# A feed-forward stream started one unit later beside the attention, with new shares of work and the other engines' part of each slice one piece later

## The chip, the cores and the metric

The kernel runs as one program on one core of a Trainium2 chip. The metric is the device time of one execution, in microseconds; the time before is the median of three runs. The engines are TensorE (PE in the profile; its weight loads are PEld), VectorE (DVE), ScalarE (ACT), GpSimd (POOL) and SyncE (SP, which only issues DMAs here). Each engine works through its own instructions in order; between engines there are semaphores, set and waited for by hand.

## The reference

The input is 8 batch entries (b = 0 to 7) of 512 tokens of width 256, fp32. Per entry four residual blocks follow each other, each on the layer norm of its input:

```
x = x + attn_a(layernorm(x))    # state-space scan: 8 heads, state 64 x 64, rotation by dt, gate, rms norm
x = x + ffn(layernorm(x))       # silu(x w1) * (x w2) -> gelu(. h1) -> gelu(. h2) -> . w3, hidden width 1024
x = x + attn_b(layernorm(x))    # delta rule: 8 heads of 32, then layer norm of its output
x = x + ffn(layernorm(x))       # the same weights again
```

The entries don't depend on each other.

## The kernel before

**Attention.** Both attention blocks work on tiles of 128 tokens, four per entry. The state-space block ("SSM stage") has 8 steps per tile, 32 in all. In a tile: transposes of the normed tile (step 0), projections (1), decay sums, angles and exponentials (2), transposes of the rotated rows (3), scores (4), products with the values and the state (5), transposes (6), output projection and residual (7). The delta block ("delta stage") has 89 steps: D1, four tiles of 5 steps (projections and Gram matrices); the inversion, 31 steps, each a product and a subtraction on VectorE alone (lines 1079 and 1081); two steps ("gap") in which the inverse goes out to DRAM and comes back as `tbd`; D2, four tiles of 9 steps, a chain of small matmuls on TensorE and small operations on VectorE. SyncE moves the Gram matrices through DRAM (`a_scr`, then `au`) ahead of the inversion, and `ti` through `t_scr` into `tbd` behind it.

**Feed-forward.** A pass `p` over one entry is two units of 256 tokens, a unit 18 slices, numbered on through the pass. In a unit: slices 0 to 7 are the first layer (w1 and w2, 8 matmuls of 256 columns each), 8 to 11 the layer h1 and 12 to 15 the layer h2 (32 matmuls each), 16 the transposes of the next unit's input (`xt`, 4), 17 the product with w3 (32). Values are split in a high and a low part, hence twice the matmuls. A slice of TensorE's work ends in one of four PSUM banks `F`. The other engines' part of it follows. For the first layer: ACT silu to `gate`, DVE product to `hid` and cast to the high part (lines 899, 903), POOL the low part `hA_lo` (line 580). For the hidden layers: ACT two gelus and the cast (702, 703, 706), POOL the low part. For slice 16: ACT and DVE make `xf_hi` and `xf_lo`. For slice 17: DVE scales and adds to x and takes its statistics (922, 925, 851). The first matmuls of a layer wait for the low parts of the layer before, its last two blocks of 128 as late as possible (line 1218 waits on `f_lo`).

**The order.** `window` weaves a stage with a stream of slices by a plan: for each step of the attention a number of slices. All engines run the same plan, so each has a fixed order. In the code the attention's operations of a step come first, then slices up to the running sum `done`. TensorE's slice s begins at position s and has its second half at s + 0.5; the other engines' part stands at s + 0.5 and is emitted as soon as `done` exceeds that:

```
def window(attention, ffn, plan):
    att, mlp, done = Steps(attention), Steps(ffn), 0
    for step, slices in enumerate(plan):
        att.before(step + 1)
        done += slices
        mlp.before(done)
```

`spread` makes a plan from shares. By it the delta plan has 15 slices in D1 (8, 2.5, 2, 2.5 by tile), 10 in the inversion, 1.5 in the gap, 9.5 in D2; the SSM plan has 36 (11.5, 6.5, 11.5, 6.5 by tile). These counts are worked out from the code.

**The loop.** SSM stage of entry 0 alone; SSM stage of entry 1 with pass 0; then for b = 1 to 6 one iteration: delta stage of entry b - 1 with pass 2b - 1 (entry b after its SSM stage), then SSM stage of entry b + 1 with pass 2b (entry b - 1 after its delta stage); then delta stages 6 and 7 with a pass each, and a last pass alone. Each window holds whole passes, so a unit's input is the result of the stage just before. SyncE issues, per iteration: load of entry b + 1 (after the store of entry b - 2 has landed), the DMAs of the delta stage, store of entry b - 1.

## Time and profile before

| | |
|---|---|
| runs | 3176.04, 3181.72, 3186.53 us; median 3181.72 |
| profiled execution, own time | 3179.42 us |
| its span, first to last instruction | 3177.4 us |
| mean granted TensorE clock | 0.891 of full speed |
| busy: PE, DVE, ACT, POOL | 78%, 47%, 36%, 29% |
| one pass of the loop (mean of 6) | 385.2 us |

The span is what the engines' records cover; the own time has some 2 us around it. A line of a window has: stretch, its length, busy us and number of instructions of PE, PEld, DVE, ACT and POOL, granted TensorE clock as a share of full speed, DMA share, GB/s. A busy share is a mean over stages with different limits, so it is read stage by stage: a window of the trace gives the busy time of each engine, the number of its instructions and the granted clock in that stretch. A wait belongs to the engine in front of it; the releaser named is the one that ended it.

### The profile page before, as it was taken

How to read it: one execution, taken by the hardware profiler on the slowest of the kernel's cores; microseconds unless marked ns; L12 is line 12 of the kernel's file. 1: busy time of each engine (PE TensorE's matmuls, PEld its weight loads, DVE VectorE, ACT ScalarE, POOL GpSimd, SP SyncE). 2: the span in 40 equal slices, each digit the busy share in tenths (PEclk: the TensorE clock that was granted, in tenths of full speed). 3: DMA queues.
4: the chain of work that ended last, by engine and by line, in shares of the span. 5: the costliest groups of instructions: out<-in, count | busy, mean ns of one | idle time of the engine just before them, and what ended most of it. 6: DMA issues, size and time to landing. Idle time of an engine off the chain costs nothing.

```text
span 3177.4 us, 54420 instructions
## 1 busy us (share of the span) xinstructions
PE 2491.4 (78%) x20928; PEld 2195.7 (69%) x20928; DVE 1483.2 (47%) x3604; ACT 1157.8 (36%) x2426; POOL 926.0 (29%) x1216
## 2 busy tenths in 40 slices
PE   4678868888688886888868888678877888777688
PEld 3567757777577775787657776568766777666578
DVE  3434553445534445444454444545444444544541
ACT  2235432445225442245412544134432354323223
POOL 2123323233223232233323223232322233233233
PEclk7679988999799997999979998789987999898799
DMA  6000000000000000000000000000000000000000
GB/s 202 1 1 1 3 12 15 1 1 18 19 7 1 1 18 21 4 1 1 20 21 3 1 8 21 14 1 1 15 14 14 1 1 10 12 15 6 21 10 7
DMA packets 86976, 43.33 MB, mean 14 GB/s; under 512 B 71472, under 2 KB 81584, under 8 KB 86704
## 3 DMA queue, kind: packets, MB, share of 16 engines
q1 hardware_dynamic: 83040, 28.12, 3.5%
q0 software_dynamic: 3664, 11.53, 1.1%
q8 instruction: 177, 2.90, 0.4%
q14 instruction: 95, 0.78, 0.1%
HBM read 27.05 MB, written 12.58 MB: 12 GB/s over the span
## 4 chain that ended last, share of the span: by engine, by line
PE 46%; DVE 25%; ACT 10%; issue 10%; POOL 5%; DMA 3%; SPq 1%; DVEq 0%; POOLq 0%; ACTq 0%
PE F L1218 21%; DVE prod L1079 4%; DVE ti L1081 3%; PE Q L1261 3%; PE F L1240 2%; PE Q L1329 2%; PE Q L1346 2%; PE Q L1308 2%; POOL hA_lo L580 2%; DVE hid L899 2%; PE Q L1444 2%; PE Q L1414 1%; PE Q L1381 1%; PE Q L1300 1%; PE Q L1312 1%
## 5 line engine op out<-in xcount | busy, mean ns | idle before, releaser
L1218 PE MATMUL F<-hA_hi,h_sb 128*128 128x256 f32 x2048 | 568.1, 311 | 107.8 <-POOL hA_lo L580 107.4
L580 POOL TENSOR_TENSOR hA_lo<-hid,hA_hi 128x256 fp32r<-128x256 f32 (+1 forms) x384 | 353.0, 920 | 879.2 <-ACT hA_hi L706 494.0
L1218 PE MATMUL F<-hA_lo,h_sb 128*128 128x256 f32 x2048 | 542.9, 299 | 0.0
L1218 PE MATMUL F<-hB_hi,h_sb 128*128 128x256 f32 x2048 | 526.1, 295 | 0.3
L1218 PEld LDWEIGHTS F<-hA_hi,h_sb 128*128 128x128 f32 x2048 | 426.6, 208 | 127.9 <-POOL hA_lo L580 115.4
L1218 PE MATMUL F<-hB_lo,h_sb 128*128 128x256 f32 x2048 | 508.8, 287 | 0.0
L1198 PE MATMUL F<-xf_hi,w_sb 128*128 128x256 f32 x1024 | 319.0, 338 | 162.6 <-DVEq L902 69.2
L1218 PEld LDWEIGHTS F<-hA_lo,h_sb 128*128 128x128 f32 x2048 | 428.3, 209 | 0.5
L1218 PEld LDWEIGHTS F<-hB_hi,h_sb 128*128 128x128 f32 x2048 | 400.8, 196 | 19.0 <-issue 15.3
L1218 PEld LDWEIGHTS F<-hB_lo,h_sb 128*128 128x128 f32 x2048 | 401.7, 196 | 0.3
L1198 PEld LDWEIGHTS F<-xf_hi,w_sb 128*128 128x128 f32 x1024 | 234.9, 229 | 183.8 <-DVEq L902 82.9
L702 ACT ACTIVATE hid<-F,sh_sb 128x256 f32<-128x256 f32 x256 | 120.9, 472 | 558.0 <-PE F L1218 557.4
L580 POOL TENSOR_TENSOR hB_lo<-hid,hB_hi 128x512 fp32r<-128x512 f32 x128 | 163.9, 1280 | 525.6 <-ACT hB_hi L706 525.6
L1198 PE MATMUL F<-xf_lo,w_sb 128*128 128x256 f32 x1024 | 302.1, 322 | 0.0
L1198 PEld LDWEIGHTS F<-xf_lo,w_sb 128*128 128x128 f32 x1024 | 237.9, 232 | 0.3
L698 ACT ACTIVATE gate<-F,s_sb 128x256 f32<-128x256 f32 x256 | 116.2, 472 | 320.0 <-POOL hA_lo L580 255.8
L899 DVE SCALAR_TENSOR_TENSOR hid<-F,s_sb,gate 128x256 f32<-128x256 f32 x256 | 123.4, 482 | 199.0 <-ACT gate L698 147.0
L1079 DVE TENSOR_TENSOR prod<-ti,au 128x31 f32<-128x31 f32 (+15 forms) x248 | 117.5, 474 | 54.2 <-DMA au<-a_scr 46.1
L1261 PE MATMUL Q<-win_sb,xT 128*128 128x512 f32 (+1 forms) x384 | 139.3, 514 | 1.9 <-ACT xT L716 1.9
L1240 PE MATMUL F<-w_sb,hA_hi 128*128 128x256 f32 x512 | 129.2, 292 | 12.8 <-POOL hA_lo L580 12.8
L1240 PE MATMUL F<-w_sb,hA_lo 128*128 128x256 f32 x512 | 124.4, 282 | 0.0
L703 ACT ACTIVATE hid<-F,sh_sb 128x256 f32<-128x256 f32 x256 | 119.3, 466 | 0.0
(212 smaller groups left out, 4492.7 us busy)
## 6 DMA issues: line engine op xcount, KB each, us to landing
h_sb<-h_dram POOLq DMA_DIRECT2D x2, 4096.0 KB, 24.5
x_sb<-x_dram SPq DMA_DIRECT2D x8, 512.0 KB, 3.9
a_scr<-q_sb SPq DMA_DIRECT2D x128, 32.0 KB, 1.7
au<-a_scr SPq DMA_DIRECT2D x8, 512.0 KB, 3.2
t_scr<-ti SPq DMA_DIRECT2D x8, 512.0 KB, 3.0
tbd<-t_scr SPq DMA_DIRECT2D x128, 32.0 KB, 1.9
out_dram<-x_sb SPq DMA_DIRECT2D x8, 512.0 KB, 3.3
w_sb<-w_dram POOLq DMA_DIRECT2D x3, 1024.0 KB, 9.0
```

The lines of the kernel that those rows point to most:

```text
L580: pool.tensor_tensor(lo, hid[:, n % 2, 0:w, :], hi.bitcast(F32), ALU.subtract).then_inc(f_lo.handle, 1)
L698: act.activation(gate[:, n % 2, :], ps[:, 0:TOK], ACT.Silu, scale=s1_sb[:, j:j + 1]).then_inc(f_act.handle, 1)
L702: act.activation(hid[:, n % 2, 0, :], ps[:, 0:TOK], ACT.Gelu, scale=scales[:, k:k + 1])
L703: own(act.activation(hid[:, n % 2, 1, :], ps[:, TOK:2 * TOK], ACT.Gelu, scale=scales[:, k + 1:k + 2]))
L899: own(dve.scalar_tensor_tensor(hid[:, n % 2, 0, :], bank_of(s)[:, TOK:2 * TOK], s2_sb[:, j:j + 1], gate[:, n % 2, :], ALU.mult, ALU.mult))
L1079: own(dve.tensor_tensor(pr, bcast(ti[:, 0:j + 1, j], 2, below), bcast(au[:, j + 1:BLK, j], 1, j + 1), ALU.mult))
L1081: own(dve.tensor_tensor(rest, rest, pr, ALU.subtract))
L1198: last = pe.matmul(ps[:, i * TOK:(i + 1) * TOK].rearrange("p (t n) -> p t n", t=2), w[:, k, j * P:(j + 1) * P], part[:, :, k, :], start=(k ...
L1218: last = pe.matmul(ps[:, i * TOK:(i + 1) * TOK], w[:, k, o:o + P], part[:, k, :], start=(i == 0 and k == 0 and part is src[0]), stop=(i == ...
L1240: last = pe.matmul(ps[:, t * D:(t + 1) * D], part[:, k, t * P:(t + 1) * P], w3_sb[:, k, :], start=(k == 0 and part is hA_hi), stop=(k == K ...
L1261: last = pe.matmul(Q[q][:, 0:c1 - c0], xT[:, k, :], win_sb[:, k, c0:c1], start=(k == 0), stop=(k == 1))
L1308: pe.matmul(Q[3][:, h * HP:(h + 1) * HP], seg[:, h, :], xdt[:, h, :], start=True, stop=True)
```

## The change

It changes order, not arithmetic. (1) The stream of units is moved by one unit against the attention. Delta stage b - 1 and SSM stage b + 1 now form one window of 121 steps with four units: the second unit of pass 2b - 2 (`rest`), both of pass 2b - 1, the first of pass 2b (`fresh`). Iteration b = 1 is written out as its own window with three units, the loop runs b = 2 to 6, delta stage 6 has three units, delta stage 7 two, and the last pass stays alone. (2) New shares, by stage and evenly inside the inversion and D2. (3) The other engines' part stands at s + 1.0 (`TAIL`), so it is emitted once `done` exceeds s + 1: with the first half of TensorE's next slice instead of with the second half of its own. (4) Since two passes are now open at once, `fmv` and `frstd` get two halves, one for SSM results and one for delta results. (5) SyncE no longer loads ahead of the delta stage: the store of entry b - 2 and the load of entry b + 1 are issued behind the first tile of `tbd`.

By the new shares, worked out from the code, the slices per stage are:

| window | D1 | inversion | gap | D2 | SSM |
|---|---|---|---|---|---|
| loop, b = 2 to 6 | 27 | 5.5 | 1.5 | 13 | 25 (4.5, 11, 4.5, 5) |
| b = 1 | 19 | 9 | 1 | 5 | 20 |
| delta 6 | 27 | 5.5 | 1.5 | 20 | |
| delta 7 | 19 | 8 | 1 | 8 | |

```diff
+TAIL = 1.0
+UNIT = [(1, 1.0)] * KT + [(0.5, 2.0)] * (2 * KT) + [(1, 0.5)] + [(0.5, 2.0)] * 2
+D2_END = D20 + D2_STEPS * NT
+SSM_END = SSM_STEPS * NT
-SSM_PLAN = spread([1, 5.9, 8.7, 3, 2, 3, 1, 0] * NT)
-DELTA_PLAN = spread([2.8, 4, 2, 2, 1] * NT + [0.5] * 8 + [0.5] * (SUB_STEPS - 9) + [6]
-                    + [2, 1] + ([1.2, 1.2] * NB + [2]) * NT)
+def shares(d1, inverse, gap, d2):
+    return ([v * d1 / (11.8 * NT) for v in (2.8, 4, 2, 2, 1)] * NT + [inverse / 10]
+            + [inverse * 0.9 / (SUB_STEPS - 1)] * (SUB_STEPS - 1) + [gap / 2] * 2 + [d2 / (D2_STEPS * NT)] * (D2_STEPS * NT))
+def ssm_shares(whole):
+    return [v * whole / (24.6 * NT) for v in (1, 5.9, 8.7, 3, 2, 3, 1, 0)] * NT
+FIRST_PLAN = spread(ssm_shares(89), UNITS)
+PEEL_PLAN = spread(shares(45, 15, 4, 20) + ssm_shares(49.5), 3)
+BODY_PLAN = spread(shares(57, 22, 5, 25) + ssm_shares(69), 4)
+LATE_PLAN = spread(shares(57, 22, 5, 49.5), 3)
+LAST_PLAN = spread(shares(45, 12, 3, 29), 2)
...
+def joined(*stages):
+    base = 0
+    for stage, first, count in stages:
+        for position in stage:
+            yield base + position - first
+        base += count
...
         done += slices
         mlp.before(done)
+    mlp.before(done + 1)
...
                     for c in range(NB):
                         sp.dma_start(tbd[BLK * c:BLK * (c + 1), :, BLK * c:BLK * (c + 1)],
                                      t_load[t, c]).then_inc(d_tbd.handle, 16)
+                    if t == 0 and late is not None:
+                        late()
...
-            with sp.Fori(1, B - 1) as b:
-                sp.wait_ge(x_loaded.handle, x_loaded.at(b, 16))
-                sp.wait_ge(x_stored.handle, x_stored.at(b - 2, 16))
-                load(b + 1)
-                delta(b - 1)
-                store(b - 1)
+            with sp.Fori(2, B - 1) as b:
+                def next_batch():
+                    store(b - 2)
+                    sp.wait_ge(x_loaded.handle, x_loaded.at(b, 16))
+                    sp.wait_ge(x_stored.handle, x_stored.at(b - 2, 16))
+                    load(b + 1)
+                delta(b - 1, next_batch)
...
-                        yield s + 0.5
+                        yield s + TAIL
...
-            with pe.Fori(1, B - 1) as b:
-                window(delta_stage(b - 1, 2 * b), ffn(2 * b - 1, b), DELTA_PLAN)
-                window(ssm_stage(b + 1, 2 * b + 1), ffn(2 * b, b - 1), SSM_PLAN)
+            def attention(b):
+                return joined((delta_stage(b - 1, 2 * b), 0, D2_END), (ssm_stage(b + 1, 2 * b + 1), 0, SSM_END))
+            def fresh(b):
+                return [(ffn(2 * b - 1, b), 0, 2 * SLICES), (ffn(2 * b, b - 1, units=(0,)), 0, SLICES)]
+            def rest(b):
+                return (ffn(2 * b - 2, b - 2, units=(1,)), SLICES, SLICES)
+            window(attention(1), joined(*fresh(1)), PEEL_PLAN)
+            with pe.Fori(2, B - 1) as b:
+                window(attention(b), joined(rest(b), *fresh(b)), BODY_PLAN)
```

The blocks of POOL, ACT and DVE change in the same way as this last part of TensorE's.

## Rows read from the trace of the kernel before

**Rows 1.** The page: TensorE's and others' busy time; the chain that ended last.

```profile
PE 2491.4 (78%) x20928; PEld 2195.7 (69%) x20928; DVE 1483.2 (47%) x3604; ACT 1157.8 (36%) x2426; POOL 926.0 (29%) x1216
...
PE 46%; DVE 25%; ACT 10%; issue 10%; POOL 5%; DMA 3%; SPq 1%; DVEq 0%; POOLq 0%; ACTq 0%
```

**Rows 2.** Windows: the loop's six iterations, delta stage 6, delta stage 7.

```profile
366.00:2677.20 2311.20, 1844.01 (x15697) 1630.01 (x15697) 1111.51 (x2700) 873.50 (x1824) 685.62 (x877) 0.90 0.04 9
2677.20:2880.80 203.60, 148.99 (x1417) 128.05 (x1417) 101.78 (x264) 57.12 (x142) 62.30 (x86) 0.89 0.05 12
2880.80:3078.00 197.20, 152.04 (x1416) 131.03 (x1417) 94.55 (x245) 58.55 (x143) 56.39 (x75) 0.87 0.05 12
```

**Rows 3.** Windows: third iteration: D1, inversion, gap, D2, SSM stage.

```profile
1137.80:1214.40 76.60, 64.09 (x433) 53.16 (x434) 30.83 (x90) 32.70 (x91) 27.67 (x28) 0.89 0.09 22
1214.40:1249.50 35.10, 17.74 (x95) 16.17 (x95) 31.50 (x74) 5.08 (x9) 4.11 (x6) 0.71 0.00 0
1249.50:1263.40 13.90, 7.87 (x87) 6.67 (x87) 5.78 (x14) 2.81 (x7) 7.08 (x12) 0.63 0.22 58
1263.40:1335.00 71.60, 61.77 (x806) 53.94 (x806) 28.96 (x82) 16.38 (x35) 22.31 (x38) 1.00 0.03 5
1335.00:1520.10 185.10, 154.75 (x1200) 140.45 (x1200) 88.19 (x193) 88.63 (x162) 53.07 (x65) 0.94 0.01 4
```

**Rows 4.** Windows: the four tiles of that SSM stage.

```profile
1335.00:1389.40 54.40, 41.88 (x294) 37.56 (x295) 26.18 (x62) 22.18 (x41) 16.61 (x23) 0.87 0.00 1
1389.40:1428.90 39.50, 37.18 (x308) 34.14 (x306) 18.90 (x37) 22.13 (x40) 10.58 (x11) 1.00 0.00 1
1428.90:1478.50 49.60, 38.44 (x296) 34.81 (x295) 22.73 (x52) 22.19 (x41) 15.19 (x19) 0.90 0.00 1
1478.50:1520.10 41.60, 37.25 (x307) 33.94 (x305) 20.38 (x42) 22.13 (x40) 10.69 (x12) 1.00 0.04 14
```

**Rows 5.** Window: line 1218 alone, two hidden slices at full clock.

```profile
1402.50:1410.30 7.80, 7.80 (x64) 7.71 (x64) 1.00 0.00 0
```

**Rows 6.** Waits of TensorE in the third iteration: us, times, longest.

```profile
PE F L1218 <- POOL hA_lo L580: 15.2, 4, 8.3
PE F L1198 <- DVEq L902: 9.2, 5, 4.2
...
PE Q L1381 <- DMA tbd<-t_scr: 5.5, 1, 5.5
PE Q L1251 <- DVE xn L858: 4.3, 1, 4.3
...
PE Q L1329 <- ACT yT L760: 4.0, 4, 1.3
...
PE Q L1300 <- ACT bT L750: 3.2, 2, 1.6
```

**Rows 7.** VectorE in the inversion: groups by line, busy us, mean ns.

```profile
L1079 DVE TENSOR_TENSOR prod<-ti,au 128x31 f32<-128x31 f32 (+15 forms) x31 | 15.2, 490 | 6.7 <-DMA au<-a_scr 5.6 <-DVE xf_lo L881 0.2
...
L899 DVE SCALAR_TENSOR_TENSOR hid<-F,s_sb,gate 128x256 f32<-128x256 f32 x3 | 1.5, 484 | 0.6 <-DVE ti L1081 0.6
```

**Rows 8.** Timeline: an inversion product beside POOL's subtraction, and the next.

```profile
1217.24 1.36 POOL L580 TENSOR_TENSOR hA_lo<-hid,hA_hi 128x512 fp32r<-128x512 f32 x1 [2.88 <-ACT hA_hi L706]
1217.52 1.37 DVE L1079 TENSOR_TENSOR prod<-ti,au 128x156 f32<-128x156 f32 x1
...
1219.27 0.48 DVE L1079 TENSOR_TENSOR prod<-ti,au 128x175 f32<-128x175 f32 x1
```

**Rows 9.** DMA issues: KB each, median us to landing.

```profile
x_sb<-x_dram SPq DMA_DIRECT2D x8, 512.0 KB, 3.9
...
tbd<-t_scr SPq DMA_DIRECT2D x128, 32.0 KB, 1.9
out_dram<-x_sb SPq DMA_DIRECT2D x8, 512.0 KB, 3.3
```

**Rows 10.** Window: the second SSM tile of entry 0, without feed-forward.

```profile
59.80:98.40 38.60, 25.26 (x124) 19.83 (x123) 15.10 (x32) 10.70 (x21) 4.67 (x6) 0.63 0.00 1
```

More of the change, by code:

```diff
@@ L54, with spread @@
 U_AHEAD, WT_AHEAD = 3, 5
-def spread(shares):
-    unit = [(1, 4)] * KT + [(0.5, 8)] * (2 * KT) + [(1, 1)] + [(0.5, 8)] * 2
-    parts = unit * UNITS
+TAIL = 1.0
+UNIT = [(1, 1.0)] * KT + [(0.5, 2.0)] * (2 * KT) + [(1, 0.5)] + [(0.5, 2.0)] * 2
+D2_END = D20 + D2_STEPS * NT
+SSM_END = SSM_STEPS * NT
+def spread(shares, units):
+    parts = UNIT * units
     total, whole = sum(c for _, c in parts), sum(shares)
@@ L201, in hybrid_kernel @@
         fbst = sb("fbst", [P, 2, 6])
-        fmv = sb("fmv", [P, NT, 2])
+        fmv2 = sb("fmv2", [P, 2, NT, 2])
         fve = sb("fve", [P, NT])
-        frstd = sb("frstd", [P, NT])
+        frstd2 = sb("frstd2", [P, 2, NT])
         in_mv = sb("in_mv", [P, NT, 2])
@@ L476, in store, with delta @@
                 sp.dma_start(x_dram(o_v, b), x_slot(b)).then_inc(x_stored.handle, 16)
-            def delta(b):
+            def delta(b, late=None):
                 for t in range(NT):
@@ L499, in delta @@
                                      t_load[t, c]).then_inc(d_tbd.handle, 16)
+                    if t == 0 and late is not None:
+                        late()
             sp.wait_ge(x_loaded.handle, 16)
             load(1)
-            with sp.Fori(1, B - 1) as b:
-                sp.wait_ge(x_loaded.handle, x_loaded.at(b, 16))
-                sp.wait_ge(x_stored.handle, x_stored.at(b - 2, 16))
-                load(b + 1)
-                delta(b - 1)
-                store(b - 1)
-            delta(B - 2)
+            sp.wait_ge(x_loaded.handle, x_loaded.at(1, 16))
+            load(2)
+            delta(0)
+            with sp.Fori(2, B - 1) as b:
[5 more added lines that the diff above has]
+                delta(b - 1, next_batch)
+            delta(B - 2, lambda: store(B - 3))
             delta(B - 1)
@@ L563, in rsqrt_ssm, with rsqrt_ffn, ffn @@
                 rsqrt(a_stats, a_stats.at(b, 1), rstd[:], ve[:], mv[:, :, 1], a_rstd)
-            def rsqrt_ffn(p, u):
+            def rsqrt_ffn(p, u, half):
                 s = slice(2 * u, 2 * u + 2)
-                rsqrt(f_stats, f_stats.at(p, u + 1), frstd[:, s], fve[:, s], fmv[:, s, 1], f_rstd)
-            def ffn(p, b, final):
-                for u in range(UNITS):
+                rsqrt(f_stats, f_stats.at(p, u + 1), frstd2[:, half, s], fve[:, s], fmv2[:, half, s, 1], f_rstd)
+            def ffn(p, b, final, units=range(UNITS)):
+                for u in units:
                     for j in range(HSLICES):
-                        yield u * SLICES + j + 0.5
+                        yield u * SLICES + j + TAIL
                         n = u * HSLICES + j
@@ L684, in xt_high, with ffn @@
                 act.copy(xf_hi[:].rearrange("p t k n -> p (t k n)"), bank_of(s)[:]).then_inc(f_xhi.handle, 1)
-            def ffn(p, b, more=True):
-                for u in range(UNITS):
+            def ffn(p, b, more=True, units=range(UNITS)):
+                for u in units:
                     s0 = u * SLICES
@@ L869, in first_delta, with norm_unit @@
                 normed(xnd[:], x_slot(b), 0, in_mv, drstd).then_inc(d_xn.handle, 1)
-            def norm_unit(p, x, u):
+            def norm_unit(p, x, u, half):
                 dve.wait_ge(f_rstd.handle, f_rstd.at(p, u + 1))
-                normed(xnf[:, 0, :], x, 2 * u, fmv, frstd)
-                normed(xnf[:, 1, :], x, 2 * u + 1, fmv, frstd).then_inc(f_xn.handle, 1)
+                normed(xnf[:, 0, :], x, 2 * u, fmv2[:, half], frstd2[:, half])
+                normed(xnf[:, 1, :], x, 2 * u + 1, fmv2[:, half], frstd2[:, half]).then_inc(f_xn.handle, 1)
             def xt_low(p, s, p_to, u):
@@ L885, in xt_low, with ffn @@
                 dve.sem_inc(f_freeV.handle, 1)
-            def ffn(p, b, final, b_next=None):
+            def ffn(p, b, final, b_next=None, half_next=0, units=range(UNITS)):
                 x = x_slot(b)
-                for u in range(UNITS):
+                for u in units:
                     s0 = u * SLICES
@@ L893, in ffn @@
                         s = s0 + j
-                        yield s + 0.5
+                        yield s + TAIL
                         if j < KT:
@@ L917, in ffn @@
                     s = s0 + W3_SLICE
-                    yield s + 0.5
+                    yield s + TAIL
                     dve.wait_ge(f_ps.handle, f_ps.at(p, s + 1))
@@ L927, in ffn @@
                         unit_stats(x, 2 * u, in_mv, d_stats)
-                if final:
-                    dve.sem_inc(x_final.handle, 1)
+                    if final and u == UNITS - 1:
+                        dve.sem_inc(x_final.handle, 1)
             def ssm_stage(b, p, next_delta=None):
@@ L1015, in ssm_stage @@
                     if t % 2:
-                        unit_stats(x, t - 1, fmv, f_stats)
+                        unit_stats(x, t - 1, fmv2[:, 0], f_stats)
                 if next_delta is not None:
@@ L1092, in normed_o @@
                     if t % 2:
-                        unit_stats(x, t - 1, fmv, f_stats)
+                        unit_stats(x, t - 1, fmv2[:, 1], f_stats)
                 for t in range(NT):
@@ L1183, in xt, with ffn @@
                 last.then_inc(f_ps.handle, 1)
-            def ffn(p, b, more=True):
-                for u in range(UNITS):
+            def ffn(p, b, more=True, units=range(UNITS)):
+                for u in units:
                     s0 = u * SLICES
```

95 lines of the change are left out of this document (59 added, 36 removed).

## The prediction

> **What bounds the kernel now.** I read the page first. TensorE is busy 78% of the span, VectorE 47%, and the chain that ended last lies 46% on TensorE and 25% on VectorE [rows 1]: TensorE sets the pace, with stretches in which it stands behind VectorE. Then the loop: six iterations take 2311.2 us, 385.2 each [rows 2]. The windows of one iteration (382.3 us, so a little short) show where TensorE is not full. It is busy 61.8 of 71.6 us in D2, but 17.7 of 35.1 in the inversion, where VectorE is busy 31.5; and in the SSM stage two tiles take 54.4 and 49.6 us where the other two take 39.5 and 41.6 [rows 3, 4]. The long tiles hold a unit's first layer, the short ones hidden layers. The waits say the same: the largest, 15.2 us, is TensorE in front of a hidden layer until POOL has made the low parts of the first layer; 9.2 us are first-layer slices behind VectorE [rows 6]. A first-layer slice is short on TensorE and long on VectorE, and the plan puts one first layer into the inversion, where VectorE is the bound, and two beside the SSM stage's long VectorE steps.
>
> **Price of a slice.** At full clock 64 matmuls of a hidden layer take 7.80 us [rows 5], 0.122 each: a hidden slice 3.9 us, a first-layer slice (8 matmuls) 1.0, the w3 slice 3.9; for slice 16 with its four transposes I take 0.6, an estimate of five such matmuls. A unit is 43.5 us of TensorE, four are 174.
>
> **Where the four units lie.** Feed-forward us on TensorE, by the slice counts of the two plans. Before: D1 35.1, inversion 15.3, gap 2.9, D2 33.8, SSM 87.0. After: D1 55.2 (a whole unit, a first layer, one hidden slice), inversion 21.5 (5.5 hidden), gap 5.9, D2 24.0 (slices 16 and 17, a first layer, three hidden), SSM 67.5 (one first layer, not two). Both sum to 174.1. Nothing is saved on TensorE; each term below is what the move does to a stage's length.
>
> **D1: +15.** It gets 20.1 us more. TensorE has 12.5 us idle of 76.6 there and a clock of 0.89 [rows 3]; I let 5 us of the new work fall into that. Bounds +10 (half fits, clock comes back) and +23 (nothing fits and the second first layer makes its own wait).
>
> **Inversion: -3.5.** No first-layer part is left on VectorE here: three products of 0.5 us, their casts, and one unit's residual and statistics, some 5.5 us of the 31.5 that are not lines 1079 and 1081 [rows 3, 7], and about 1 us of waits. But 5.5 hidden slices bring as many POOL subtractions of 1.36 us. One of them stands beside a product that took 1.37 us, where the next, larger one took 0.48 [rows 8]: about 0.9 us lost each, 5 in all, of which this stage pays some 2 already. So -6.5 + 3. Bounds -6.5 and 0. The Trainium skill has the rule (SBUF — State Buffer, "SBUF: two separate sides"): a VectorE operation with two SBUF inputs and a GpSimd operation lock one port pair for the whole instruction and the other waits. The trace agrees with 1.37 against 0.48 us; by the rule in full every subtraction costs up to its own length, 7.5 us, and the stage gains nothing. TensorE's 21.5 us of hidden slices have the inversion and both DMA chains to lie in, so they are no bound even where half of them run at the half clock (1.2 GHz) seen here (0.71 on the mean of the stage).
>
> **Gap: +4.** Between the landing of `tbd` (5.5 us of wait now, [rows 6]) and D2 the plan puts 5.9 us where 2.9 stood, and TensorE comes out of an idle stretch at a clock of 0.63 [rows 3]. +3 at full clock, +6 at half. SyncE's moved store and load stand behind the first tile of `tbd`: 3.3 us for the store to land, then the load of 3.9, and the second tile's transfers of 1.9 behind them [rows 9], about 9 us. That tile is wanted at D2's step 3, which is form, 5.9 us of slices and three steps away, some 14 us. So nothing; without that cover up to 4 us, once per iteration. The load itself is wanted at D2's end.
>
> **D2: -5.3.** 9.8 us of slices leave. TensorE's own waits there are 9.8 us in 71.6; the chain alternates between it and VectorE, so with thinner filling some of VectorE's latency shows, and one first layer adds 8 products and casts, 6.6 us, to a VectorE that the chain needs. I give back 4.5. Bounds -9.8 and 0.
>
> **SSM stage: -33.** By tile. Tile 1 took 39.5 us; its plan has 4.5 hidden slices, 16 and 17, so 22.1 us; 17.4 remain, of which 2.3 are waits of the kinds in [rows 6] and 15.1 attention at full clock. Tile 0 took 54.4, of which 3.0 are before its first transpose; of 51.4, 21.5 are slices and 15.1 attention, so 14.8 go to the first layer; 7.6 of that (half of 15.2) is the wait on POOL at the layer's end. After: tiles 0 and 2 have 4.5 hidden slices each, 17.6 + 15.1, and thinner cover in steps 0, 4 and 5, where the plan now has 0, 0 and half a slice; I take 4.2 us of waits, an estimate: one of about 0.9 and two near the longest of today, 1.6 (what `yT` and `bT` cost now is 7.2 for the stage [rows 6]): 36.9 each. Tile 1 has the first layer spread over four steps: 16.2 + 15.1 + 7 = 38.3. Tile 3: 16.2 + 15.1 + 3.5 = 34.8. With 5 at the seam (3 now, 2 more since the last step of D2 has no slice; the wait there is 4.3 [rows 6]) the stage is 151.9, against 185.1. Bounds: 147 and 171 (rival B). Can a tile be so short? Alone it takes 38.6 us at a clock of 0.63 with 25.3 of TensorE [rows 10]; at full clock those halve, which leaves a chain of some 26 to 29 us: yes, but not by much.
>
> **Part one piece later: +3.** A layer's first matmuls need the last low part of the layer before. Where that now stands behind one more attention step, TensorE may wait; against it, attention results no longer wait behind ScalarE's gelus. 12 layer starts in four units; 0.25 us each. Bounds -5 and rival C. The bank rotation has four banks, so a part 1.5 slices behind frees its bank in time; the second halves of `fmv` and `frstd` cost no instruction.
>
> **Sum.** An iteration: 15 - 3.5 + 4 - 5.3 - 33 + 3 = -19.8, five times -99. Iteration b = 1 (48.0 us of slices in the SSM stage against 87.0, 44.5 in D1, 19.5 in D2, the first layer still in the inversion): +7 - 1 + 1 - 8 - 45 + 2 = -44. Delta stage 6, 203.6 us now [rows 2], gets a third unit: +15 - 3.5 + 4 + 12 + 0.5 = +28, with 48.0 us of slices in D2 against 33.8. Delta stage 7, 197.2: +4. First and last windows: 0. Together -111: span 3177.4 - 111 = 3066.4. The profiled execution's own time is 2.0 above its span and the median 2.3 above that, so 3071 us, 3.5% less.
>
> **Rivals.** A is this forecast, own range 3000 to 3140; chance 0.65.
> B, the gain is eaten by the SSM chain: no tile gets below the 39.5 us of today's shortest, and the one with the first layer keeps its 7.6 us wait, 47.1. Stage 170.6, 18.5 more in each of six iterations, 111 in all: 3182, no change. For it: chain operations on VectorE and ScalarE are most of a tile. Against it: today's short tiles are 94% full on TensorE, not chain-bound [rows 4]. 0.08.
> C, slower: the later part leaves TensorE waiting at each layer start. Place: lines 1218 and 1240 behind POOL's low parts. Today's mean of such waits in this iteration is 15.2 / 4 = 3.8 us; at 3.3 for each of the 84 layer starts in the windows (28 units) it is 277 us, less the 21 counted: 3327. It decides from 1.6 us a start on. Against it: the last two blocks are waited for late, and the layer start inside a step has a half slice of 1.6 us or more in front. 0.10.
> D, more: cover everywhere. D1 +10, inversion -5.5, gap +3, D2 -9.8, SSM -36 are -38, five times -190, with -52 for b = 1 and +20 for delta 6: -222, so 2960. The Trainium skill (TensorE: Matmul & The Clock Gate, "HAM oscillation") has idle gaps put the clock down, so fewer gaps pay twice; the trace agrees, 1.00 in the filled tiles and 0.87 and 0.90 in those with the wait [rows 4]. 0.17.
>
> **Range and chances.** 0.3% is about what a measurement here can tell from no change. Faster 0.82 (A, D), within 0.3% 0.07 (most of B), slower 0.11 (C and a rest). From 2950 (past D) to 3165 (A's edge and half the way to B) no more than 2 in 10 is left out.
>
> **What the profile of the changed kernel would show.** Iterations of about 365 us; D1 near 92; an inversion without lines 899 and 903, near 32, with single products of 1.3 us beside POOL; SSM tiles of 35 to 38 with a clock near 1.00, the second the longest; TensorE's wait on POOL at line 1218 well under 15 us an iteration; its wait for `tbd` longer than 5.5. I am wrong if tiles stay at 39.5 or more, if D1 grows by over 20, or if lines 1218 and 1240 wait at every layer.

## The result, and the profile after

The changed kernel takes 3247.04 us (median of three runs, 3246.8 to 3249.94) against 3181.72: the ratio is 1.0207, with a 95% interval of 1.0193 to 1.0221. It is slower by 2.1%, where the prediction said 3071 us and 3.5% faster, and it lies outside the range. The profiled execution spans 3248.2 us, 70.8 more than before.

From the page, the busy times and the chain that ended last (the same lines of before are [rows 1]):

```profile
PE 2483.8 (76%) x20897; PEld 2181.8 (67%) x20928; DVE 1491.6 (46%) x3604; ACT 1168.4 (36%) x2434; POOL 929.3 (29%) x1216
...
PE 47%; DVE 25%; ACT 9%; issue 8%; POOL 6%; DMA 3%; SPq 1%; DVEq 0%; ACTq 0%; POOLq 0%
```

The same work is in a longer span, so the 70.8 us are waits of the pace-setting engine, or a slower clock. Read the windows as in [rows 2]. They are, in this order: the first window (SSM stage of entry 1 with pass 0) with all before it; iteration b = 1; the loop; delta stage 6; delta stage 7 with the last pass.

```profile
1.00:394.50 393.50, 266.77 (x1686) 230.12 (x1693) 153.63 (x346) 130.70 (x247) 91.13 (x146) 0.78 0.13 41
394.50:757.70 363.20, 278.75 (x2257) 241.08 (x2261) 174.21 (x428) 127.37 (x269) 97.65 (x128) 0.85 0.03 7
757.70:2708.40 1950.70, 1510.86 (x13060) 1328.28 (x13080) 934.70 (x2251) 741.54 (x1530) 569.54 (x731) 0.91 0.04 9
2708.40:2943.50 235.10, 185.94 (x1772) 164.80 (x1772) 114.40 (x287) 75.22 (x177) 79.14 (x102) 0.92 0.05 12
2943.50:3248.20 304.70, 241.44 (x2124) 217.57 (x2124) 114.65 (x294) 93.58 (x211) 91.62 (x109) 0.88 0.05 11
```

Before, the loop began at 366.0 us and its six iterations took 2311.2; here iteration b = 1 and the loop's five take 363.2 + 1950.7 = 2313.9. So the balance is +28.5 before the first delta stage, +2.7 in the six iterations, +31.5 in delta stage 6 (203.6 before) and +8.1 behind it (296.6 before): together the 70.8.

One iteration, the third of the loop's five (delta stage 3), by stage, and then its four SSM tiles, to be laid beside [rows 3, 4]. The SSM stage is cut here at its first transpose, 3.0 us later than in [rows 3]; by this cut before had 74.6 us in D2 and 182.1 in the SSM stage.

```profile
1541.80:1638.00 96.20, 83.88 (x631) 73.44 (x632) 42.20 (x110) 43.87 (x111) 37.48 (x39) 0.96 0.06 12
1638.00:1669.00 31.00, 13.70 (x115) 13.30 (x113) 28.84 (x62) 5.85 (x12) 5.67 (x5) 0.79 0.00 1
1669.00:1686.50 17.50, 10.72 (x111) 9.83 (x112) 1.97 (x5) 3.67 (x9) 5.16 (x9) 0.68 0.35 106
1686.50:1760.90 74.40, 55.33 (x722) 47.22 (x722) 38.41 (x110) 12.97 (x27) 21.47 (x41) 0.92 0.03 5
1760.90:1930.30 169.40, 136.38 (x1037) 120.02 (x1041) 75.55 (x166) 82.10 (x148) 44.30 (x55) 0.94 0.00 1
```

```profile
1760.90:1808.10 47.20, 37.28 (x262) 32.66 (x264) 15.78 (x34) 21.75 (x39) 11.40 (x15) 0.84 0.00 1
1808.10:1853.10 45.00, 34.42 (x255) 30.26 (x255) 24.16 (x55) 19.76 (x36) 12.77 (x18) 0.92 0.00 1
1853.10:1891.50 38.40, 33.00 (x270) 29.52 (x270) 16.64 (x36) 20.00 (x36) 10.61 (x13) 1.00 0.00 1
1891.50:1930.30 38.80, 31.68 (x255) 27.58 (x254) 18.97 (x41) 20.59 (x37) 9.52 (x11) 1.00 0.01 2
```

The inversion is the stage that came out as thought: 31.0 us, VectorE busy with its 62 own instructions and nothing else. D1 grew by 19.6 us, more than the SSM stage gave back (12.7), and the first two SSM tiles are 10.2 and 6.7 us over the forecast.

TensorE's waits over the whole execution (us, times, longest):

```profile
PE Q L1454 <- DMA tbd<-t_scr: 161.0, 8, 23.5
PE F L1291 <- POOL hB_lo L617: 75.0, 33, 6.9
PE F L1271 <- DVEq L961: 56.3, 29, 5.8
PE Q L1324 <- DVE xn L917: 47.6, 7, 20.4
PE F L1313 <- POOL hA_lo L617: 43.5, 15, 6.7
PE F L1291 <- POOL hA_lo L617: 41.2, 18, 9.0
```

The wait on `hB_lo`, in front of layer h2, is new: the view of before has no such line. The waits on POOL's low parts at a layer's start (lines 1291 and 1313, which were 1218 and 1240) come to 159.7 us; before they were 107.4 and 12.8. The first matmuls in D2 wait up to 23.5 us for `tbd`, 161.0 us over the eight delta stages where before it was 44.8 in all: the inversion's hidden slices run out early. Where the new wait is from, the timeline shows, 24.6 us into that SSM stage (start, duration, engine, line):

```profile
1776.84 1.28 ACT L783 ACT_TABLE_LOAD   x1
...
1778.75 1.28 ACT L786 ACT_TABLE_LOAD   x1
...
1781.26 1.28 ACT L750 ACT_TABLE_LOAD   x1
...
1782.92 0.47 ACT L751 ACTIVATE hid<-F,sh_sb 128x256 f32<-128x256 f32 x1
1783.50 0.62 ACT L754 CAST hB_hi<-hid 128x512 fp32r<-128x512 f32 x1
1784.20 1.26 POOL L617 TENSOR_TENSOR hB_lo<-hid,hB_hi 128x512 fp32r<-128x512 f32 x1 [2.31 <-ACT hB_hi L754]
...
1785.51 0.58 PE L1291 MATMUL F<-hB_hi,h_sb 128*128 128x256 f32 x1 [6.93 <-POOL hB_lo L617]
```

TensorE was in the first slice of h2 and lacked only its last two blocks, which come from h1's last slice. ScalarE's gelus of that slice stand, by the new order, behind the angles and exponentials of the SSM tile's step 2. The chain gelu, cast, subtraction begins too late, and TensorE stands 6.9 us. Much of what ScalarE does in that time is to change its function table: three loads of 1.28 us each, for the sine (line 783), the exponential (786) and the gelu (750).

In the first window, whose plan has the same slices in every tile, the late part can be read by itself. From 180 us on, before and after:

```profile
180.00:366.00 186.00, 157.38 (x1204) 142.41 (x1204) 86.69 (x190) 89.11 (x163) 52.80 (x64) 0.92 0.00 1
180.00:394.50 214.50, 166.45 (x1201) 151.56 (x1205) 86.42 (x190) 86.39 (x161) 56.37 (x69) 0.86 0.00 1
```

Of the 28.5 us, 13.1 are waits for POOL at layer starts (28.0 us for 14.9), and TensorE's same matmuls are busy 9.1 us longer at the lower clock. The rest lies in other waits.

### The profile page after: what moved, and what is told of

Same layout as the page of the kernel before. It is cut to its first block, busy times and chain, and to the rows that moved or that the text cites. A ratio compares the mean times of both kernels' runs of the same rounds, so it can differ in the third digit from the quotient of the medians.

```text
span 3248.2 us, 54000 instructions
## 1 busy us (share of the span) xinstructions
PE 2483.8 (76%) x20897; PEld 2181.8 (67%) x20928; DVE 1491.6 (46%) x3604; ACT 1168.4 (36%) x2434; POOL 929.3 (29%) x1216
## 4 chain that ended last, share of the span: by engine, by line
PE 47%; DVE 25%; ACT 9%; issue 8%; POOL 6%; DMA 3%; SPq 1%; DVEq 0%; ACTq 0%; POOLq 0%
PE F L1291 18%; DVE prod L1138 4%; PE Q L1334 4%; DVE ti L1140 3%; PE F L1271 3%; POOL hA_lo L617 3%; PE F L1313 3%; PE Q L1419 3%; PE Q L1381 2%; PE Q L1402 2%; PE Q L1517 2%; DVE hid L958 1%; PE Q L1454 1%; POOL rn L661 1%; PE Q L1385 1%
## 5 line engine op out<-in xcount | busy, mean ns | idle before, releaser
L1291 PE MATMUL F<-hA_hi,h_sb 128*128 128x256 f32 x2048 | 532.9, 299 | 44.5 <-POOL hA_lo L617 41.2
L1291 PE MATMUL F<-hA_lo,h_sb 128*128 128x256 f32 x2048 | 514.2, 289 | 0.0
L1291 PEld LDWEIGHTS F<-hA_lo,h_sb 128*128 128x128 f32 x2048 | 408.6, 199 | 0.3
L1271 PE MATMUL F<-xf_hi,w_sb 128*128 128x256 f32 x1024 | 288.2, 315 | 65.9 <-DVEq L961 56.3
L1271 PE MATMUL F<-xf_lo,w_sb 128*128 128x256 f32 x1024 | 272.0, 299 | 0.0
L1271 PEld LDWEIGHTS F<-xf_hi,w_sb 128*128 128x128 f32 x1024 | 211.8, 207 | 83.6 <-DVEq L961 63.6
L750 ACT ACTIVATE hid<-F,sh_sb 128x256 f32<-128x256 f32 x256 | 121.9, 476 | 306.2 <-PE F L1291 304.8
L1271 PEld LDWEIGHTS F<-xf_lo,w_sb 128*128 128x128 f32 x1024 | 213.6, 209 | 0.5
L1454 PE MATMUL Q<-tbd,uw 128*32 128x128 f32 x1024 | 43.8, 324 | 161.0 <-DMA tbd<-t_scr 161.0
L1454 PEld LDWEIGHTS Q<-tbd,uw 128*32 128x32 f32 x1024 | 32.1, 128 | 164.7 <-DMA tbd<-t_scr 162.7
```

What stands on the lines that cost most here:

```text
L750: act.activation(hid[:, n % 2, 0, :], ps[:, 0:TOK], ACT.Gelu, scale=scales[:, k:k + 1])
L1271: last = pe.matmul(ps[:, i * TOK:(i + 1) * TOK].rearrange("p (t n) -> p t n", t=2), w[:, k, j * P:(j + 1) * P], part[:, :, k, :], start=(k ...
L1291: last = pe.matmul(ps[:, i * TOK:(i + 1) * TOK], w[:, k, o:o + P], part[:, k, :], start=(i == 0 and k == 0 and part is src[0]), stop=(i == ...
L1454: last = pe.matmul(Q[1][r, o:o + P], uw[:, t, h, 1 - i, :], tbd[:, h, :], start=True, stop=True)
```

## The experiments

Stage lengths of one iteration of the loop, from each trace: D1 begins at the first transpose of the delta stage, the inversion is from its first product to its last subtraction, D2 begins at the first block subtraction behind `tbd`, the SSM stage at its first transpose. All times are in us; "first" is all before the first delta stage. The stages are those of one profiled execution, the ratio is that of medians, against runs of the kernel before taken beside it. Where the loop's iterations differ, a mean or a range stands.

| kernel | ratio (95%) | first | b = 1 | D1 | inv. | gap | D2 | SSM (tiles) | iteration | delta 6 |
|---|---|---|---|---|---|---|---|---|---|---|
| before | 1 | 366.0 | 386.0 | 77 | 35.9 | 14.5 | 76 | 182 (51.5 39.5 49.6 41.7) | 385.2 | 203.6 |
| after | 1.0207 (1.0193-1.0221) | 394.5 | 363.2 | 97 | 31.0 | 17.5 | 74.6 | 169 (47.1 45.0 38.7 38.8) | 390.1 | 235.1 |
| e1 | 1.012 (1.0099-1.0141) | 362.9 | 362.2 | 94 | 31.1 | 17.0 | 84.7 | 165 (41.5 46.3 38.7 38.2) | 391 | 235.1 |
| e2 | 1.0383 (1.0361-1.0406) | 391.9 | 401.8 | 78 | 35.4 | 13.6 | 74.6 | 201 (53.0 47.1 51.4 49.5) | 402.8 | 202.1 |
| e3 | 0.995 (0.9931-0.997) | 365.3 | 356.6 | 77 | 35.2 | 13.5 | 74.1 | 182 (51.7 39.3 49.7 41.6) | 382.0 | 234.4 |
| e4 | 1.0044 (1.0026-1.0061) | 375.4 | 355.6 | 95 | 31.1 | 17.4 | 77 | 165 (41.8 45.0 38.4 38.8) | 383-388 | 231.8 |
| e5 | 1.0267 (1.0245-1.0289) | 395.7 | 363.2 | 98.6 | 35.0 | 18.0 | 76.8 | 164 (37.8 48.0 39.5 38.9) | 389-393 | 236.8 |
| e6 | 1.0175 (1.0154-1.0196) | 394.1 | 366.4 | 90 | 34.8 | 17.5 | 74.7 | 170 (47.1 45.0 38.7 38.8) | 386-388 | 235.0 |
| e7 | 1.0262 (1.024-1.0283) | 391.7 | 362.8 | 100 | 31.1 | 17.7 | 78.6 | 165 (38.0 49.2 39.4 38.5) | 392.5 | 238.1 |
| e8 | 1.0202 (1.0179-1.0224) | 373.2 | 358.5 | 80 | 36.3 | 16.8 | 83.2 | 173 (51.3 37.7 37.0 46.5) | 389.1 | 255.1 |
| e9 | 0.9942 (0.9926-0.9959) | 366.4 | 356.0 | 77 | 35.2 | 13.5 | 74.2 | 182 | 382.3 | 231.1 |
| e10 | 0.9956 (0.9937-0.9976) | 363.7 | 361.1 | 94 | 31.1 | 16.9 | 74.6 | 162 (38.2 48.9 37.0 38.2) | 378.9 | 231.3 |
| e11 | 1.0097 (1.0076-1.0118) | 363.3 | 361.2 | 95 | 35.4 | 17.7 | 81.0 | 160 (37.3 45.7 37.2 39.9) | 389.1 | 234.4 |
| e12 | 1.0225 (1.0204-1.0245) | 365.4 | 361.2 | 94-97 | 31.1 | 17.0 | 63 | 191 (54 46 50 42) | 395-400 | 231.4 |
| e13 | 0.9986 (0.9975-0.9997) | 366.7 | 356.0 | 94 | 31.1 | 17.0 | 74.8 | 165-169 (below) | 382-386 | 231.6 |
| e14 | 1.0126 (1.0099-1.0152) | 365.6 | 355.9 | 94 | 33.1 | 22.0 | 81.7 | 159 (37.3 45.7 37.3 38.2) | 389.1 | 235.0 |

### The three parts apart: e1, e2, e3

e1 is the changed kernel with `TAIL = 0.5`.

> The changed kernel with the other engines' part of a slice back at s + 0.5 (new order and new shares kept). Theory T, the late part: in the changed kernel TensorE stands behind POOL's last low part wherever a layer starts behind a long attention step (6.9 and 4.3 us in one iteration's SSM stage, 9.0, 5.7, 7.7 and 5.7 in the first window). With the part early again the first window gives back its 28 us and each of the six iterations some 15, delta stages 6 and 7 together about 10: near 3120 us, ratio to the kernel before 0.98. Rival S, the shares: the 23 us wait for tbd and the fuller D1 are the cost, the late part only hurts the first window: about 3220, ratio 1.012.

Measured 3220.79 us. The first window goes back from 394.5 to 362.9 us, the SSM stage from 169 to 165; D2 grows from 74.6 to 84.7. So the late part costs at layer starts, and in D2 it pays. By time it is the rival's case, 3220 and 1.012: taking the late part away leaves a kernel that is still slower than before, so shift and new shares together cost 1.2% when the part is early.

e2 is the kernel before with only the late part:

```diff
         mlp.before(done)
+    mlp.before(done + 1)
...
-                        yield s + 0.5
+                        yield s + 1.0
```

> The kernel before with only the other engines' part moved from s + 0.5 to s + 1.0; order and shares of before. Theory T: each of the seven windows with an SSM stage beside a whole pass gets the 28 us that the first window of the changed kernel got, so 3180 + 200 = 3380 us. Rival: the first window's 28 us come from the longer program or another side effect of the change, not from the late part: 3180.

Measured 3305.83 us, the slowest of all. Here the edit is alone, and its price plain: 26 us in the first window, 19 in every SSM stage. It is less than the 28 per window of the expectation, and far from its rival, no change. The tiles with hidden slices pay nearly all of it (39.5 to 47.1, 41.7 to 49.5), those with a first layer 1.5 and 1.8 us. Waits of TensorE in it:

```profile
PE F L1219 <- POOL hA_lo L581: 129.4, 18, 9.3
PE F L1219 <- POOL hB_lo L581: 78.4, 14, 5.6
```

The second line is new, 5.6 us twice in each of the seven SSM stages beside a pass, in the tiles with hidden slices. The first had 107.4 us before.

e3 is the shift by one unit alone, `TAIL = 0.5` and the shares of before (delta stage 6 gets its third unit by the same shares):

```diff
-TAIL = 1.0
+TAIL = 0.5
-BODY_PLAN = spread(shares(57, 22, 5, 25) + ssm_shares(69), 4)
+BODY_PLAN = old(OLD_DELTA, 2) + old(OLD_SSM, 2)
```

> The feed-forward stream one unit later, but with the shares of before and the part at s + 0.5. A unit is 18 slices, so each stage has the same kinds of slices as before. Theory T: the shift alone costs nothing and takes away only waits on a result just made: an iteration within 5 us of 385, total 3150 to 3190 with the edges. Rival M, the shift or its moved DMAs cost: iterations over 390, total over 3210.

Measured 3165.6 us, ratio 0.995. What iteration b = 1 gives (29 us) delta stage 6 takes (31). The loop's iteration is 382.0 us against 385.2, and that is no new speed: one iteration of before, the one in [rows 3], already took 382.4, with 1.2 to 1.8 us less in the gap and 1.4 less in D2 than its neighbours. Under the shift all five are of this kind. The expectation (3150 to 3190) held.

e1 and e3 differ in nothing but the shares, so the three parts can be put in a row: the shift 3182.6 to 3165.6, the new shares from there to 3220.8 (+55 us), the late part from there to 3247.0 (+26). With the part early it is the new shares, meant to save time, that cost most.

### Where the late part costs and where it pays: e4, e9, e10

e4 keeps the late part except for the slices at a layer's end:

```diff
-                        yield s + TAIL
+                        yield s + (0.5 if j in (KT - 1, KT + KT // 2 - 1, HSLICES - 1) else TAIL)
```

> The changed kernel, the part at s + 1.0 except for the last slice of each layer (7, 11 and 15 of a unit), which is back at s + 0.5. Theory T says that only the last low part of a layer matters: within 15 us of the run with all parts at s + 0.5, near 3120. If instead the late part costs everywhere (banks, the double buffer hid), it stays nearer to the changed kernel: over 3190.

Measured 3197.46 us: the three slices in eighteen that end a layer carry 47 us of span. The first window goes from 394.5 to 375.4, SSM tile 0 from 47.1 to 41.8 in most iterations. The expectation was 3120, within 15 us of e1. It is 23 us faster than e1, since D2 keeps most of the late part and stays at 77 us. The rest of the miss is that of e1, the shares.

e10 is the changed kernel with the late part in the steps of D2 only (0.5 elsewhere), e9 the same with the shares of before.

```diff
-        mlp.before(done)
+        mlp.before(done - (0.5 if others and len(plan) > SSM_END and step in LATE else 0))
```

> The changed kernel (new shares), the part at s + 1.0 in D2 only, s + 0.5 elsewhere. Theory G: D2 goes from the 85.9 us of the run with all parts early back to 75, while the first window (340 us long up to the first delta stage's start at 363) and the SSM stage (164.6) stay short: an iteration 381, total 3248 - 28 - 50 - 15, about 3150. Rival, D2's length follows from its slices and not from the part's place: 3220 as in that run.

> The run with the shift alone (shares of before, part at s + 0.5; 3165.6 us), with the part at s + 1.0 in the steps of D2 only. Theory G, the late part hurts where a layer starts behind a long attention step (SSM stage) and helps where the attention itself is a chain of short steps (D2): D2's 74.1 us become 73, an iteration 381, total about 3155. Rival: late is late everywhere, each layer start in D2 waits too: over 3175.

e10 takes 3161.25 us, ratio 0.9956; e9 3160.49, 0.9942. So with the late part in D2 alone the new shares (e10) and the old ones (e9) take the same time. From after to e10 the span falls by 94 us (3248.2 to 3154.1; by medians 86, for e10's profiled execution is the fastest of its seven): 31 in the first window, 56 in the five iterations. TensorE's waits on POOL at layer starts fall by 98, from 159.7 to 62.1 (32.7, 27.1 and 2.3 us). In D2 the late part pays 10 us an iteration under the new shares (84.7 to 74.6) and nothing under the old (74.1 and 74.2). D2 of one iteration in e1 and in e10:

```profile
1647.30:1733.20 85.90, 62.50 (x727) 52.97 (x722) 38.41 (x110) 14.67 (x30) 24.39 (x47) 0.80 0.03 4
```

```profile
1624.40:1699.00 74.60, 56.26 (x726) 47.95 (x722) 38.38 (x110) 13.02 (x27) 23.07 (x46) 0.89 0.03 5
```

The same matmuls take 62.5 and 56.3 us: over half of the difference of 11.3 goes with the clock. That VectorE's first-layer parts stood ahead of the chain's small operations is how I read the rest; it wasn't measured alone, nor which of the two brought the other.

### Other places for the slices: e5, e6, e7, e8, e11, e12

e5, e6 and e7 change `BODY_PLAN` alone and have the late part everywhere. e5 gives the inversion 3 slices more and the gap 2, out of D2 (3) and the SSM stage (2); e6 moves one from D1 into the inversion; e7 moves 2.5 from the SSM stage into D2.

```diff
-BODY_PLAN = spread(shares(57, 22, 5, 25) + ssm_shares(69), 4)
+BODY_PLAN = spread(shares(57, 30, 5, 25) + ssm_shares(61), 4)        # e5
+BODY_PLAN = spread(shares(52.5, 26.5, 5, 25) + ssm_shares(69), 4)    # e6
+BODY_PLAN = spread(shares(57, 22, 5, 35) + ssm_shares(59), 4)        # e7
```

> The changed kernel with one share moved in the loop: 8 of the 69 units of share of the SSM stage go to the inversion (22 to 30), about 7.8 us of TensorE's slices per iteration; everything else as changed. In the changed kernel TensorE stands 23 us before tbd, so the inversion takes them for nothing. Theory F, a tile of the SSM stage has a floor set by its own chain (tiles of 38 to 40 us with 16 to 18 us of slices): the stage's 169.5 us shrink by no more than 3. Rival P, the SSM stage is TensorE's: it shrinks by about 8.

> The changed kernel with one hidden slice (4 us) moved in the loop from D1 to the inversion. Theory F: D1 is TensorE's, its 96.6 us shrink by 4, inversion, gap and D2 keep their lengths, an iteration 385. Rival: D1's waits on VectorE and ScalarE, not TensorE, set its length, nothing changes.

> The changed kernel with 10 units of share (about 10 us of slices) moved in the loop from the SSM stage to D2 (25 to 35, as much as D2 had before the change). Theory F: D2 is a chain with a floor, and with thin filling the granted clock falls (0.92 in the changed kernel, 1.00 before): D2 stays at 74 to 76 us with its clock back near 1.00, so what the change took out of D2 bought nothing. Rival P, D2 is TensorE's: it grows to about 84.

None beats 1.0175, and no expectation was met in full: e5's SSM stage gave 5 us, between theory and rival, and e7's D2 took 78.6 us at a clock of 0.92. e6 gives a price: one hidden slice out of D1 is worth 7 us there (97 to 90), of which 3.9 are matmuls; but the last first-layer part then falls into the inversion, 31.0 to 34.8. e5 pays the same 4 us there, 2 in D1 and 2 in D2, for 5 in the SSM stage; e7 pays 3 in D1 and 4 in D2 for 4. A slice can't be moved alone: the edges of the first layers move with it. In e5 SSM tile 0 took 37.8 us with as many slices and the late part: none of its layer starts waited for POOL.

e8 starts the stream of a pass at slice 10, so that hidden slices fall elsewhere, with shares of its own and early parts at layer ends as in e4:

```diff
+CUT = 10
+PEEL_PLAN = spread(shares(12, 28, 4.5, 34) + ssm_shares(26.5), 0, 36 + CUT)
+BODY_PLAN = spread(shares(36.5, 32, 4.5, 34) + ssm_shares(71), CUT, 72)
```

> A new version made from what the runs showed: the loop's window begins at slice 10 of a pass instead of slice 18, so that eight hidden slices fall exactly on the inversion, D1 has 16 slices (36 us, as before the change, not 55), D2 14.5 (33 us) and the SSM stage 31.5 (70 us); the part at s + 1.0 except at a layer's last slice. Theory F: D1 77 us, inversion 31, gap 16, D2 76, SSM 168 (two tiles with a first layer at 46, two at 38), an iteration near 368 against 385 before and 389 changed: near 3080 us, ratio 0.968. If the position of the slices doesn't matter, only their sum, it is at 3200 like the run with the same parts.

Measured 3242.47 us for an expected 3080. D1 has 80 us, the inversion 36.3 although eight hidden slices lie beside it, but the first layers now sit in D2 (83.2) and in two SSM tiles (51.3, 46.5), and delta stage 6 grows to 255. The two tiles without one are at 37.7 and 37.0.

e11 and e12 are e10 with other shares in the loop. e11 has 8 slices in the inversion instead of 5.5 and half a slice more in the gap, one each fewer in D1, D2 and the SSM stage. e12 has 2 slices in D2 and no first layer, and 36 in the SSM stage as before.

```diff
-BODY_PLAN = spread(shares(57, 22, 5, 25) + ssm_shares(69), 4)
+BODY_PLAN = spread(shares(52.5, 31, 4.5, 25) + ssm_shares(65), 4)    # e11
+BODY_PLAN = spread(shares(57, 22, 5, 4.5) + ssm_shares(89.5), 4)     # e12
```

> As the run with the part late in D2 only, with other shares in the loop: D1 26 slices, the inversion all 8 hidden slices that lie there, the gap slices 16 and 17, D2 12, the SSM stage 24. Theory F: TensorE's wait for tbd (23 us) takes 10 us of slices for nothing; D1 4 to 5 us shorter, the SSM stage at its floor of 164, an iteration 377, total about 3130. Rival, as in the two runs that gave the inversion more: what D1 gives, the inversion takes (3.8 us there): no shorter than 3150.

> As the run with the part late in D2 only, but in the loop D2 has only slices 16 and 17 (4.5 us of TensorE's work instead of 24) and the SSM stage 36 slices with two first layers as before the change. Theory H, D2 has a floor set by its own chain and a first layer stretches it: without any D2 is 60 to 65 us (64.7 in the written-out iteration with five hidden slices), the SSM stage 182, an iteration near 387. Rival, D2 is at its floor at 74 whatever it holds: 74, and an iteration of 397.

e12, whose theory for D2 held, bounds the price of a first layer on D2's chain: 63 us with two slices, 74.6 with thirteen, the first layer among them (in iteration b = 1 of after, five slices and no first layer took 64.6). D2 of its third loop iteration (61.5 us; 64.6 in two of the others):

```profile
1663.80:1725.30 61.50, 39.52 (x563) 30.70 (x563) 30.30 (x88) 3.73 (x11) 13.77 (x34) 0.72 0.03 6
```
In the SSM stage the eleven slices cost more: 162 to 191 us, with the tiles back at 54 and 50. e11 loses more in the inversion (35.4) and in D2 (81.0) than it gains in the SSM stage, and takes 3209.69 us for an expected 3130.

### The best of both, twice: e13, e14

e13 is e10 with the first window, iteration b = 1 and the window of delta stage 7 in the shares of before (in the first window they give the same slices per tile). e14 has besides one slice more in the inversion and one in the gap, out of D2 and the SSM stage (its expectation says out of D1; by the plan D1 keeps its 27).

```diff
-FIRST_PLAN = spread(ssm_shares(89), UNITS)
-PEEL_PLAN = spread(shares(45, 15, 4, 20) + ssm_shares(49.5), 3)
-LAST_PLAN = spread(shares(45, 12, 3, 29), 2)
+FIRST_PLAN = old(OLD_SSM, 2)
+PEEL_PLAN = old(OLD_DELTA, 2) + old(OLD_SSM, 1)
+LAST_PLAN = old(OLD_DELTA, 2)
...
-BODY_PLAN = spread(shares(57, 22, 5, 25) + ssm_shares(69), 4)
+BODY_PLAN = spread(shares(57, 26, 5, 25) + ssm_shares(65), 4)        # e14 only
```

> The new shares in the four passes of the loop, the feed-forward stream one unit later, the late part in D2 alone, and the old shares in the written-out iteration and in the window of delta stage 7. Theory: the two gains add up, because they sit in different windows: loop iteration 378.9 us as where the late part was confined to D2, written-out iteration 356 and last window 294.6 us as under the old shares; together about 3147 us, ratio 0.990. Rival: the passes of the stream end at other places where shares change from one window to the next, so that a first layer meets D2 at the seam; then the written-out windows give nothing back and the ratio stays at 0.995 to 0.996.

> As the kernel beside it, but in the loop the inversion has 6.5 hidden slices instead of 5 at the cost of one and a half slices in D1, so that TensorE has work in the 23 us in which it waits for tbd. Theory: D1 falls by 7 us a slice, the last part falls into the inversion and costs about 3.8 us, so an iteration of 375 to 378 us and a ratio of 0.986 to 0.989. Rival: the first layers move earlier into D2's chain and give it all back: iteration 379 to 386 us, ratio 0.990 to 1.00.

e14 takes 3210.96 us, 1.0126, above even its rival's 1.00: with two slices put into TensorE's wait for `tbd` the first layer behind them moved forward in D2; inversion 31.1 to 33.1, gap 17 to 22, D2 74.8 to 81.7. e13 gives 0.9986. The two windows returned what was expected (b = 1 from 361.1 to 356.0, delta stage 7 with the last pass from 303.6 to 293.6), and yet the time is not 3147 but 3173.82: the loop, whose plan and order are word for word those of e10, takes 382 to 386 us an iteration instead of 378.9. The SSM tiles of one iteration in e10 (the third of the loop's five, and all five are alike) and in e13 (the fourth):

```profile
1699.00:1737.20 38.20, 33.69 (x262) 29.25 (x263) 15.85 (x34) 21.45 (x39) 11.94 (x15) 0.95 0.00 1
1737.20:1786.10 48.90, 39.58 (x256) 35.12 (x255) 24.17 (x55) 19.87 (x36) 12.67 (x17) 0.83 0.00 1
1786.10:1823.10 37.00, 32.89 (x272) 29.45 (x271) 16.65 (x36) 21.31 (x39) 10.25 (x12) 1.00 0.00 1
1823.10:1861.30 38.20, 32.00 (x256) 27.66 (x254) 20.31 (x42) 19.59 (x35) 9.38 (x11) 1.00 0.01 2
```

```profile
2086.50:2128.20 41.70, 38.12 (x262) 33.73 (x264) 15.78 (x33) 21.54 (x39) 11.79 (x14) 0.83 0.00 1
2128.20:2177.00 48.80, 39.32 (x255) 35.16 (x255) 24.18 (x55) 19.87 (x36) 12.68 (x17) 0.83 0.00 1
2177.00:2217.30 40.30, 37.38 (x271) 33.78 (x271) 16.65 (x36) 21.55 (x39) 10.27 (x12) 0.87 0.00 1
2217.30:2255.50 38.20, 31.81 (x255) 27.64 (x255) 20.35 (x42) 19.34 (x35) 9.56 (x11) 1.00 0.01 2
```

The same instructions take 38.2 us at a clock of 0.95 and 41.7 at 0.83, 37.0 at 1.00 and 40.3 at 0.87. So a tile of the same order can take two lengths about 3.5 us apart, and within e13 it changes from one iteration to the next: tile 0 took 38.2, 41.7, 38.2, 41.7 and 41.7 us. It changes from one execution to the next as well. e10's seven took 3155.9 to 3163.1 us five times, and 3173.4 and 3175.8 twice at a lower mean clock (0.882 and 0.881 for 0.885 to 0.888). If its windows outside the loop kept their length, the slowest had 383 us an iteration (an estimate), near the mean of 383.7 in e13's trace. e13's twelve lie between 3162.6 and 3178.7, so the slower kind is the usual one there and the rarer one in e10; whether the edit to the other windows does this isn't shown. Differences between kernels here of up to 7 us an iteration, some 1% of the time, may be this and no merit of the shares. So e3, e9 and e10 (0.994 to 0.996) can't be told apart, and that they beat the kernel before by their order isn't shown either.

## Why the prediction was wrong

**What was right.** Stage lengths here and below are those of the third iteration on either side, where nothing else is said. The inversion: -4.1 measured for -3.5, with lines 899 and 903 (now 958 and 962) gone from it, and beside POOL's 1.46 and 1.33 us subtractions VectorE's took 1.29 and 1.33 us. The gap: +3.6 for +4. Delta stage 6: +31.5 for +28. The wait at the seam between D2 and the SSM stage: 5.2 us for 5. TensorE's wait for `tbd` grew, as named. SSM tile 2, 38.4 (37.0 in e10) for 36.9, a near hit that tile 3, 4 us over, shows to be partly luck. The moved store and load cost nothing that the waits show. The tell-tale signs against the forecast were named too: tiles of 39.5 or more, D1 over +20 (+19.6 here, +20.1 on the loop's mean).

**Step "Part one piece later: +3", and "first and last windows: 0".** This is the step with the wrong idea. I priced a layer start at 0.25 us, against which rival C stood with 3.3 at all 84 starts. The mechanism is C's, but at few places: where the layer's last part falls behind a long attention step there is a new wait of 5.6 to 6.9 us, elsewhere of 1 to 2 or none. In the first window four waits of 9.0, 5.7, 7.7 and 5.7 us stand where before there were two of 8.1 and 6.5; it grew by 28.5 us, and e1, with the part early and nothing else changed, takes 31.6 back. My count for C, 84 starts, had left this window out: with its six there are 90. The wait of 4.3 us in SSM tile 1 isn't from the late part, since e10 has it too. The pure edit, e2, costs 3.8%. In the new shares it costs 0.9% net (1.0207 over 1.012), since in D2 it gives 10 us an iteration back. My argument against C, that the last two blocks are waited for late, holds for the TensorE side; the late thing was ScalarE's queue, where half a slice of delay became a whole attention step of exponentials. The edit is stated in slices, but its delay is that of whatever attention step stands between.

**Step "SSM stage: -33".** By the cut at the transpose -35.2 was forecast and -12.7 came, the largest miss: 22.5 us an iteration. Tile 0: 47.1 for 36.9. Without the late part it is 41.7 at the low clock (e13) and 38.2 at the higher (e10), so about 5.5 us go with the wait on `hB_lo` (6.9 by the view) and 3.5 with the clock. Tile 1: 45.0 for 38.3; the first layer spread over it needs 7 us more than I took from [rows 4], and no run of the loop got below 44.8. Tile 3: 38.8 for 34.8 with nothing but attention's own waits. In the loops with other shares than before, the tiles with 3.5 to 5.5 slices and no first layer lie mostly between 37 and 40 us with no order by their number, where their matmuls need some 31 to 33 (the lowest is 35.4 in e8; tile 0 took 41.4 to 44.8 in e1, e4 and in part of e13 without the wait on `hB_lo`). That is rival B's mechanism, with a floor nearer 37 than its 39.5. The forecast had taken 26 to 29 us for the chain alone, by halving the 25.3 us of matmuls in [rows 10]. At that stretch's own clock of 0.63 full speed leaves 15.9 of them, so 29 is the better figure, itself an estimate. e9 and e10 show what the shorter stage was worth in the whole: old shares and new take the same time.

**Step "D1: +15".** +19.6. I let 5 us of the new work fall into idle time; none did: TensorE is idle 12.3 us there, 12.5 before. The clock even rose (0.89 to 0.96, a gain that I had not in the sum), and 3 of the 19.6 are the late part (94 us in e1 and e10). D1 was full: e6 shows 7 us for a slice of 3.9.

**Step "D2: -5.3".** By the same cut -3.3 was forecast and -0.2 came. 9.8 us of slices left and the stage stayed. TensorE's busy time fell by 6.4 us only, at a clock of 0.92 where it had been 1.00. What left were hidden slices, which had lain in the shadow of the chain, and a first layer came that lies on it: with eleven slices fewer, the first layer among them, the stage has 63 us (e12).

**Sum.** In the loop's third iteration: 4.6 (D1) - 0.6 - 0.4 + 3.1 (D2) + 22.5 (SSM), less the 3 that I had given the late part, are 26.2 us. On the mean of the loop it is 24.9 (five iterations took 1925.2 us before, 1950.7 after, forecast -99), so 124.5; b = 1 gave -22.8 for -44, 21.2; the first window 28.5; delta stage 6 3.5; behind it 4.1. Together 181.8, which is 3248.2 less the forecast span of 3066.4. By cause: 94 us are the late part outside D2 (after against e10). Of the other 88, 68 lie in e10's loop, most of it in the SSM stage (162.3 us for 146.9 forecast by this cut, in each of five iterations), and 19 in b = 1.

**What stays open.** Whether the shift with any shares is truly faster than before: the best runs, 0.9942 to 0.9956, lie within what the two lengths of a tile make. What makes a stretch take the longer or the shorter of its two lengths wasn't isolated. How much of D2's length is VectorE's first-layer parts and how much the clock is argued, not shown.
